# Summing attention rows: GpSimd folds to 16 columns, VectorE adds the rest, and five engines' instruction lists in a new order

## The chip, the cores and the metric

The kernel runs on one core of one Trainium2 chip. The metric is the device time of that core in microseconds (us). An execution is judged as a whole: there is one launch, and every input starts in device memory.

## The reference

128 graphs of 128 nodes with 384 features go through two layers, each with a residual and a layer norm.

```
# L0, twice:  u_left = h (h Wl^T)^T / sqrt(384),  u_right likewise with Wr
#             u = u_left*triu(adj) + u_right*triu(adj,1)^T
#             att = exp(u)*adj / (sum(exp(u)*adj) + 1e-10)
#             h = relu(layer_norm(att @ (h Wlin^T + b)))
x = layernorm(x + L0(x))
# L1, 12 heads of 32:  q,k,v = x Wq^T, x Wk^T, x Wv^T + bv
scores = q k^T * scale + (adj + adj)
row_nonzero = any(scores != 0, axis=-1)          # else the row becomes 0
out = nan_to_num(softmax(scores)) v  @ Wo^T + bo
x = layernorm(x + out)
```

Every product is made of three products of halves (high times high, high times low, low times high), so that 16-bit operands carry nearly full precision. Each value that feeds TensorE is therefore rounded by ScalarE (`_hi`) and its rest is taken by VectorE or GpSimd (`_lo`).

## The kernel before

The 128 graphs are taken in 32 groups of four (`GROUP`). One pass of the program (`body(p)` on each engine) works on L0 of group `it` and on L1 of group `it - 1` at once, and on the last head block, the last output projection and the last layer norm (`TAIL`) of the group before that. Passes 0, 1 and 2 stand as straight code, passes 3 to 30 are a loop of seven rounds with four passes each, and passes 31 to 33 are straight code again. Pass 0 has no L1 work and also rounds weights 2 to 9 (`setup`); pass 32 has only L1 work, pass 33 only the tail.

Each engine has its own list of calls in `body`, written out; an engine does its list strictly in order and meets the others only through semaphores, whose counts `upto` works out. A call is named by its stage and its part:

- L0: `nl(l, c)` the six products of the left and right weights for layer l (nine matmuls of 512 columns each); `hl(l, b)` the linear part of graph b (nine of 384); `u(l, h)` the pair scores of two graphs (18 matmuls of 256 columns); `u_add`, `exp_u`, `weigh`, `round_e`, `e_rest` make the attention weights `e`; `ctx(l, b)` multiplies them on; `den`, `bn`, `z_variance`, `z_power`, `inv_std`, `norm_z` normalise layer 0's result `z`; `th(k)` turns it (four 128x128 transposes).
- L1: `x1t` turns the residual `x1`, `qk(c)` and `v(b)` are projections, `scores(b, c)` the head scores of graph b. On TensorE these are 36 small matmuls per graph into the four banks 4 to 7. VectorE's `scores(b, j)` (line 847) adds the adjacency, writes the negated scores `s` and takes their minimum `nmax`; ScalarE's `exps(b, j)` (line 597) makes the exponentials `w`. Then `pt` (transposes of `w`, three per graph), `pv` (36 matmuls of 33 columns), `rs_of` and `pv` on VectorE (lines 874, 877, 889: divide by the row sum into `o`), `to` (transposes of `o`) and `po` (output projection), and `po_stats`, `y2_power`, `fin` for the last layer norm.

The reference sets a row to zero when all its scores are zero. The kernel tests this by two numbers of each row and head: the maximum, and the sum of `s` over its 128 columns (`total`). GpSimd's `folds(b)` (lines 455 to 473) makes the sum: seven additions of halves, 128 columns to 64, 32, 16, 8, 4, 2 and 1, for 12 heads at once, each waiting for the one before by a semaphore (`fold1` to `fold6`, `s_tot`). VectorE's `live_of(b)` (line 865) takes the larger of the maximum and `total` into `live`, and `rs_of(b)` multiplies the reciprocal by whether that is above zero (line 877). VectorE's `scores(b)` for b of 2 and 3 waits for `fold1` of two graphs earlier, since `s` has two buffers.

The eight PSUM banks are shared by a written list `BANK_USES`: bank by bank, in which order the stages use it. Before a stage writes its bank, TensorE waits in `await_bank` for the last reader of the stage ahead of it in that list (`READ`: for `pt` the rest `pt_lo`, for `pv` the output `o_ok`, and so on). `scores` of a graph waits for all four banks 4 to 7 at its first call. So a reader that comes late on VectorE holds TensorE at the next use of the bank.

The DMA issues (SyncE) are: inputs of the next group, `adj2` for L1, `xres` for the residual, and the stores of finished rows. Their order is the same in both kernels.

Of the kernel before, what the change touches and what calls it, by code (L numbers as in the profile page):

```python
# [5 lines left out]
GROUP = 4  # L6
# [24 lines left out]
def program(nc, x, xT, adj, adjT, weights, biases, ln_cols, ln_rows, out):  # L31
# [5 lines left out]
    with ExitStack() as stack:  # L37
# [62 lines left out]
        def signal(name, per_group):  # L100
# [12 lines left out]
            for p in ("u_full", "u_read", "u_sum", "e_raw", "e_ok", "e_hi_ok", "e_lo_ok"))  # L113
# [16 lines left out]
        fold1, fold2, fold3, fold4, fold5, fold6, s_tot = (  # L130
            signal(p, GROUP) for p in ("fold1", "fold2", "fold3", "fold4", "fold5", "fold6", "s_tot"))
# [15 lines left out]
                     s_full, s_ok, s_tot, fold1, fold2, fold3, fold4, fold5, fold6, p_ok, pt_full, pt_hi, pt_lo, pv_full, live_ok, rcp_ok,  # L147
# [9 lines left out]
        def uses(*runs):  # L157
# [3 lines left out]
            uses(("nl0", 1), ("hl0", 2), ("v", 0), ("pt", 1), ("pv", 0), ("nl1", 4), ("to", 1), ("pv", 2), ("c1", 0)),  # L161
            uses(("to", 3), ("qk", 1, 5), ("th", 1), ("nl1", 0), ("to", 0), ("pt", 5, 6), ("to", 2), ("c1", 1)),
            uses(("pv", 3), ("nl0", 3), ("u0", 1), ("qk", 0, 3), ("th", 0), ("v", 3), ("pt", 0), ("nl1", 2),
                 ("po", 0), ("pv", 1), ("hl1", 1), ("po", 1), ("pt", 10)),
            uses(("nl0", 4), ("x1t", 0), ("qk", 4), ("v", 1), ("th", 2), ("nl1", 3), ("hl1", 0), ("pt", 7),
                 ("u1", 1), ("hl1", 3), ("c1", 2)),
            uses(("hl0", 1), ("x1t", 1), ("c0", 0, 2), ("s", 0), ("v", 2), ("s", 4, 8), ("pt", 4), ("s", 12),
                 ("pt", 8), ("hl1", 2), ("po", 2), ("c1", 3)),
            uses(("nl0", 2), ("hl0", 0), ("x1t", 2), ("c0", 1, 3), ("s", 1, 5), ("nl1", 1), ("s", 9, 13), ("u1", 0)),
            uses(("nl0", 5), ("u0", 0), ("hl0", 3), ("s", 2, 6), ("pt", 2), ("s", 10), ("nl1", 5), ("s", 14),  # L170
                 ("pt", 9)),
            uses(("nl0", 0), ("po", 3), ("qk", 2), ("s", 3, 7), ("pt", 3), ("s", 11, 15), ("pt", 11)))
# [14 lines left out]
        class Pass:  # L187
# [40 lines left out]
            def await_bank(self, eng, stage, *parts):  # L228

                last = {}  # L230
# [102 lines left out]
        def _(pool):  # L333
# [115 lines left out]
            def folds(p, b):  # L449
# [32 lines left out]
            def body(p):  # L482
# [3 lines left out]
                hl(p, 0, 1)  # L486
                out_bias(p, 0)
                weigh(p, 0, 0)
                e_rest(p, 0, 0)
                weigh(p, 0, 1)  # L490
                hl(p, 0, 2)
                e_rest(p, 0, 1)
                out_bias(p, 1)
                hl(p, 0, 3)
                out_bias(p, 2)
                y2_power(p, 3)
                scale_adj(p)
                z_power(p, 0)
                out_bias(p, 3)
                v(p, 0)  # L500
                folds(p, 0)
                folds(p, 1)
                v(p, 1)
                xt(p, 0)
                v(p, 2)
                folds(p, 2)
                xt(p, 1)
                hl(p, 1, 0)
                y2_power(p, 0)
                folds(p, 3)  # L510
                hl(p, 1, 1)
                weigh(p, 1, 0)
                v(p, 3)
                weigh(p, 1, 1)
                e_rest(p, 1, 0)
                e_rest(p, 1, 1)
# [18 lines left out]
        def _(act):  # L535
# [142 lines left out]
            def body(p):  # L678
                nl(p, 0, 0)
                setup(p, 2)  # L680
                setup(p, 3)
                setup(p, 4)
                nl(p, 0, 1)
# [4 lines left out]
                nl(p, 0, 5)  # L688
                x1_norm(p, 2)
                x1_norm(p, 3)  # L690
                hl(p, 0, 0)
# [3 lines left out]
                x1t(p, 1)  # L695
                x1t(p, 2)
                round_e(p, 0, 0)
                exp_u(p, 0, 1)
                fin(p, 2)
                hl(p, 0, 2)  # L700
                qk(p, 0)
                round_e(p, 0, 1)
                hl(p, 0, 3)
                ctx(p, 0, 0)
                qk(p, 1)
                ctx(p, 0, 1)
# [5 lines left out]
                setup(p, 5)  # L712
                qk(p, 5)
                setup(p, 6)
                v(p, 0)
                th(p, 0)
                th(p, 1)
                exps(p, 0, 0)
                exps(p, 0, 1)
                exps(p, 0, 2)  # L720
                th(p, 2)
                exps(p, 0, 3)
                exps(p, 1, 0)
                pt(p, 0, 0)
                exps(p, 1, 1)
# [3 lines left out]
                pt(p, 1, 0)  # L729
                setup(p, 7)  # L730
                nl(p, 1, 1)
                xt(p, 0)
                exps(p, 1, 2)
                nl(p, 1, 2)
                setup(p, 8)
                setup(p, 9)
                v(p, 1)
                fin(p, 3)
                v(p, 2)
                nl(p, 1, 3)  # L740
                to(p, 0)
                exps(p, 1, 3)
                xt(p, 1)
                pt(p, 1, 1)
# [46 lines left out]
        def _(dve):  # L791
# [293 lines left out]
            def body(p):  # L1085
# [3 lines left out]
                scale_z(p, 1)  # L1089
                nl(p, 0, 0)  # L1090
                pv(p, 3)
                nl(p, 0, 1)
                scale_z(p, 2)
                scale_z(p, 3)
                inv_std(p, 1)
                to(p, 3)
                shift_z(p, 0)
# [451 lines left out]
```

## Time and profile before

| | us |
|---|---|
| median of 3 runs | 2906.12 |
| lowest, highest | 2905.11, 2912.86 |
| the profiled execution | 2910.63 |
| its span, first to last instruction | 2908.9 |
| TensorE busy | 2811.0 |
| VectorE busy | 2433.9 |
| ScalarE busy | 1773.5 |
| GpSimd busy | 1662.0 |
| mean granted TensorE clock | 0.987 of full speed |

"Busy" is the time in which an engine has an instruction at work; instructions that only wait, branch or issue transfers don't count. The profile page lists this first, then the span in slices, the queues, the chain of work that ended last, and the costliest groups of instructions with the idle time of the engine ahead of each and what ended it. A matmul's recorded length is longer than the distance to the next one, since they overlap; where the speed of TensorE matters, the distances count.

### The profile page before, as it was taken

How to read it: one execution, taken by the hardware profiler on the slowest of the kernel's cores; microseconds unless marked ns; L12 is line 12 of the kernel's file. 1: busy time of each engine (PE TensorE's matmuls, PEld its weight loads, DVE VectorE, ACT ScalarE, POOL GpSimd, SP SyncE). 2: the span in 40 equal slices, each digit the busy share in tenths (PEclk: the TensorE clock that was granted, in tenths of full speed). 3: DMA queues.
4: the chain of work that ended last, by engine and by line, in shares of the span. 5: the costliest groups of instructions: out<-in, count | busy, mean ns of one | idle time of the engine just before them, and what ended most of it. 6: DMA issues, size and time to landing. Idle time of an engine off the chain costs nothing.

```text
span 2908.9 us, 74992 instructions
## 1 busy us (share of the span) xinstructions
PE 2811.0 (97%) x24768; PEld 1794.6 (62%) x24768; DVE 2433.9 (84%) x8042; ACT 1773.5 (61%) x4107; POOL 1662.0 (57%) x2097
## 2 busy tenths in 40 slices
PE   7999999999999999999999999999999999999996
PEld 4566666666666566665666656666566656666654
DVE  4888988888888789887888878897888888888886
ACT  4565666556676556665566655566565666655664
POOL 2555566556565556664565645656555655556564
PEclk9999999999999999999999999999999999999997
DMA  4001011101011010111110110101101011101000
GB/s 149 30 31 45 21 45 42 42 32 45 21 42 42 32 45 21 45 42 38 36 42 24 43 43 31 45 21 46 39 34 43 31 35 42 42 31 45 21 27 21
DMA packets 56061, 113.03 MB, mean 39 GB/s; under 512 B 4944, under 2 KB 37712, under 8 KB 55632
## 3 DMA queue, kind: packets, MB, share of 16 engines
q1 hardware_dynamic: 55632, 107.76, 11.0%
q8 instruction: 214, 3.51, 0.5%
q14 instruction: 215, 1.76, 0.2%
HBM read 82.58 MB, written 25.17 MB: 37 GB/s over the span
## 4 chain that ended last, share of the span: by engine, by line
PE 80%; DVE 10%; issue 6%; ACT 3%; DVEq 0%; POOL 0%; DMA 0%; SPq 0%; POOLq 0%; ACTq 0%
PE psum L1251 58%; PE psum L1261 9%; PE psum L1312 9%; PE psum L1405 3%; DVE z L1017 2%; PE psum L1379 1%; ACT w L597 1%; DVE nT_lo L814 1%; DVE rs L877 1%; DVE pT_lo L812 1%; DVE hT_lo L1038 1%; DVE o L889 1%; ACT qk_hi L537 1%; ACT pT_hi L537 1%; DVE st L916 1%
## 5 line engine op out<-in xcount | busy, mean ns | idle before, releaser
L597 ACT ACTIVATE w<-s,nmax 128x128 f32<-128x128 f32 x1536 | 479.4, 401 | 1.9 <-DVE nmax L847 1.9
L1251 PE MATMUL psum<-hT_hi,w_hi 128*128 128x512 f16 x1152 | 442.8, 384 | 35.4 <-issue 19.7
L1251 PE MATMUL psum<-hT_hi,w_lo 128*128 128x512 f16 x1152 | 442.3, 384 | 0.0
L1251 PE MATMUL psum<-hT_lo,w_hi 128*128 128x512 f16 x1152 | 442.2, 384 | 0.0
L537 ACT ACTIVATE nT_hi<-psum 128x512 f16<-128x512 f32 x384 | 230.1, 599 | 306.1 <-PE psum L1251 306.1
L847 DVE CUSTOM_DVE_ANT_0 s<-psum,adj 128x128 f32<-128x128 f32 x1536 | 350.6, 285 | 33.3 <-PE psum L1379 30.6
L464 POOL TENSOR_TENSOR fold<-fold 128x384 f32<-128x384 f32 (+4 forms) x640 | 344.0, 538 | 50.2
L464 POOL TENSOR_TENSOR fold<-s 128x768 f32<-128x768 f32 x128 | 244.2, 1908 | 194.7 <-DVE nmax L847 194.7
L388 POOL TENSOR_TENSOR hl_lo<-hl_raw,hl_hi 128x384 fp32r<-128x384 f32 x256 | 246.6, 968 | 144.9 <-ACT hl_hi L537 140.7
L812 DVE TENSOR_TENSOR pT_lo<-psum,pT_hi 128x512 f16<-128x512 f32 x384 | 251.5, 683 | 35.1 <-ACT pT_hi L537 34.7
L537 ACT ACTIVATE pT_hi<-psum 128x512 f16<-128x512 f32 x384 | 221.7, 596 | 84.3 <-PE psum L1261 84.3
L814 DVE SCALAR_TENSOR_TENSOR nT_lo<-psum,nT_hi 128x512 f16<-128x512 f32 x384 | 256.3, 681 | 12.4 <-ACT nT_hi L537 12.3
L431 POOL TENSOR_TENSOR yrstd<-yvar,pw 128x4 f32<-128x4 f32 x32 | 32.4, 1013 | 397.8 <-DVE yvar L997 397.8
L537 ACT ACTIVATE z<-psum,rden 128x384 f32<-128x384 f32 x256 | 138.3, 579 | 197.4 <-DVE rden L963 197.4
L1251 PE MATMUL psum<-w_hi,hT_lo 128*128 128x384 f16 x768 | 250.3, 326 | 0.0
L1251 PE MATMUL psum<-w_lo,hT_hi 128*128 128x384 f16 x768 | 250.3, 326 | 0.0
L1251 PE MATMUL psum<-w_hi,hT_hi 128*128 128x384 f16 x768 | 250.3, 326 | 0.0
L1251 PE MATMUL psum<-xT_hi,w_hi 128*128 128x512 f16 x576 | 219.8, 382 | 0.0
L1251 PE MATMUL psum<-xT_lo,w_hi 128*128 128x512 f16 x576 | 219.1, 380 | 0.0
L1251 PE MATMUL psum<-xT_hi,w_lo 128*128 128x512 f16 x576 | 218.8, 380 | 0.0
L1251 PEld LDWEIGHTS psum<-hT_hi,w_hi 128*128 128x128 f16 x1152 | 113.2, 98 | 165.1 <-issue 43.0
L1261 PE MATMUL psum<-ident,w 128*128 128x128 f32 x1536 | 208.7, 276 | 2.6 <-DVE nmax L847 2.0
(133 smaller groups left out, 8066.6 us busy)
## 6 DMA issues: line engine op xcount, KB each, us to landing
xTin<-xT SPq DMA_DIRECT2D x32, 768.0 KB, 4.5
xres<-x SPq DMA_DIRECT2D x32, 768.0 KB, 4.6
out<-y SPq DMA_DIRECT2D x128, 192.0 KB, 1.9
adjn<-adj SPq DMA_DIRECT2D x32, 256.0 KB, 4.8
adjT_sb<-adjT SPq DMA_DIRECT2D x32, 256.0 KB, 5.0
adj<-adj SPq DMA_DIRECT2D x32, 256.0 KB, 2.7
x<-weights SPq DMA_DIRECT2D x4, 576.0 KB, 5.3
s<-weights SPq DMA_DIRECT2D x3, 576.0 KB, 6.3
```

The costliest lines, as they stand in the source:

```text
L388: nc.gpsimd.tensor_tensor(hl_lo[:, b, 0:FEAT], hl_raw[:, b], hl_hi[:, b, 0:FEAT].bitcast(f32), ALU.subtract).then_inc(hlr_lo[l].sem, 1)
L464: nc.gpsimd.tensor_tensor(fold[:, :, 0:n], src[:, :, 0:n], src[:, :, n:2 * n], ALU.add)\
L537: return nc.scalar.activation(dst, src, ACT.Copy, scale=scale)
L597: last = nc.scalar.activation(w[:, m], s[b % 2][:, m], ACT.Exp, bias=nmax[b % 2][:, m:m + 1], scale=-1.0)
L812: nc.vector.tensor_tensor(dst, src, rounded, ALU.subtract).then_inc(done.sem, 1)
L814: nc.vector.scalar_tensor_tensor(dst, src, scale, rounded, ALU.mult, ALU.subtract)\
L847: last = nc.vector.tensor_tensor_reduce(out=s[b % 2][:, m], in0=psum[:, SC[j], c * TOK:(c + 1) * TOK], in1=adj2[:, b], scale=-1.0 / TEMPER ...
L1017: nc.vector.tensor_scalar(z[:, b], z[:, b], rstd[0][:, b:b + 1], nmr[:, b:b + 1], ALU.mult, ALU.add)\
L1251: last = mm(dst, a, b, start=(i == 0), stop=(i == total - 1))
L1261: last = transpose(dst[:, n * 128:(n + 1) * 128], src, ident[:])
L1312: last = mm(dst, a, m, start=(i == 0), stop=(i == len(terms) - 1))
L1405: last = mm(dst[:, n * VCOL:(n + 1) * VCOL], a, m, start=(i == 0), stop=(i == 2))
```

## The change

`folds(b)` keeps its first three additions (128 columns to 64, 32, 16) and loses the four small ones. VectorE's `live_of(b)` waits for `fold3` and adds the 16 columns left in one `tensor_reduce` over 12 heads, then waits for that and goes on as before. GpSimd's own wait for `s_tot` ahead of its next `folds` stays, and now is released by VectorE.

```diff
@@ folds (GpSimd)
-                for n, src_ok, done in ((TOK // 2, None, fold1), (TOK // 4, fold1, fold2), (TOK // 8, fold2, fold3),
-                                        (TOK // 16, fold3, fold4), (TOK // 32, fold4, fold5),
-                                        (TOK // 64, fold5, fold6)):
+                for n, src_ok, done in ((TOK // 2, None, fold1), (TOK // 4, fold1, fold2), (TOK // 8, fold2, fold3)):
...
-                pool.wait_ge(fold6.sem, p.upto(fold6, b + 1))
-                if b >= 2:
-                    pool.wait_ge(live_ok.sem, p.upto(live_ok, b - 1))
-                elif p.before.l1:
-                    pool.wait_ge(live_ok.sem, p.before.upto(live_ok, b + 3))
-                nc.gpsimd.tensor_tensor(total[b % 2][:], fold[:, :, 0], fold[:, :, 1], ALU.add)\
-                    .then_inc(s_tot.sem, 1)
@@ live_of (VectorE)
+                dve.wait_ge(fold3.sem, p.upto(fold3, b + 1))
+                nc.vector.tensor_reduce(total[b % 2][:], fold[:, :, 0:TOK // 8], AX.X, ALU.add).then_inc(s_tot.sem, 1)
                 dve.wait_ge(s_tot.sem, p.upto(s_tot, b + 1))
@@ scores (TensorE): the wait for qk's rests joins the bank wait of c == 0
-                    p.await_bank(pe, "s", *range(TILES * b, TILES * (b + 1)))
-                if b == 0:
+                    p.await_bank(pe, "s", *range(TILES * b, TILES * (b + 1)), also=(("qk", 1),) if b == 0 else ())
+                elif b == 0:
                     pe.wait_ge(qkr_lo.sem, p.upto(qkr_lo, 2 * c + 2))
```

All four compute engines' lists in `body` and `BANK_USES` are laid out anew; the calls are the same calls. TensorE's list, before and after (parts in brackets, `p` left out):

```
before: nl00 pv3 nl01 nl02 to3 nl03 nl04 po3 nl05 hl00 hl01 u00 u01 x1t0-2 hl02 hl03 qk0 qk1 ctx00 ctx01 qk2
        ctx02 ctx03 qk3 qk4 qk5 v0 th0 sc0(0-2) th1 v1 v2 v3 th2 sc1(0-2) pt00 pt01 nl10 nl11 pt02 pt10 nl12 pv0
        nl13 sc2(0-2) to0 nl14 pt11 pt12 po0 nl15 pv1 hl10 sc3(0-2) to1 hl11 pt20 pt21 pt22 u10 po1 pv2 u11
        pt30 to2 hl12 pt31 hl13 pt32 po2 ctx10-13
after:  nl00 pv3 nl01 nl02 to3 nl03 nl04 nl05 po3 hl00 u00 hl01 u01 hl02 x1t0-2 hl03 qk0 ctx00 ctx01 qk1
        ctx02 ctx03 qk2 qk3 qk4 qk5 th0 th1 v0 sc0(0,1) th2 sc0(2) v1 v2 v3 sc1(0-2) pt00 pt01 nl10 pt02 nl11
        pv0 nl12 sc2(0-2) to0 nl13 pt10 pt11 pt12 nl14 po0 nl15 pv1 pt20 sc3(0-2) hl10 pt21 u10 hl11 pt22 hl12
        pt30 to1 pt31 pv2 u11 pt32 hl13 to2 po1 po2 ctx10-13
```

VectorE's list in the stretches that matter, after (before where it differs in kind):

```
start:   rs3 z_variance1 scale_z0 nl00 pv3 scale_z1 nl01 inv_std1 scale_z2 to3 ...   (before: scale_z1 ahead of nl00)
z:       bn00 den01 bn01 bn02 bn03 z_variance0 qk1 qk2 fin3 inv_std0 norm_z0-3 qk3 qk4 qk5 th0 v0 th1 sc00-03
         (before: ... z_variance0 qk2 qk3 qk4 fin3 inv_std0 norm_z0-3 qk5 v0 sc00-03 th0)
head 1:  v1 v2 v3 th2 sc10 sc11 pt00 pt01 pt02 sc12 live0 rs0 sc13 pv0 nl10 nl11 sc20 sc21 sc22 to0 sc23 nl12
         pt10 pt11 pt12 live1 po0 nl13 nl14 po_stats0 rs1 nl15 pt20 pv1 hl10 sc30 sc31 sc32 u10 sc33 live2 ...
```

ScalarE: `th0 th1 th2` now follow `qk5` directly, ahead of `v0` and of the `exps` of graph 0 (before, `th2` came between them); `exps` of graph 1 follow `pt0x`; `v1`, `v2`, `v3` and `xt2` stand together after `to0`. GpSimd: `weigh` and `e_rest` of both halves are paired, `z_power(0)` is ahead of `y2_power(3)`, `v3` and `xt2` come earlier.

## Rows read from the trace of the kernel before

**Rows 1.** The page's part 1: busy time and share of the span per engine.
```profile
PE 2811.0 (97%) x24768; PEld 1794.6 (62%) x24768; DVE 2433.9 (84%) x8042; ACT 1773.5 (61%) x4107; POOL 1662.0 (57%) x2097
```
**Rows 2.** Busy by stretch: length; PE, PEld, DVE, ACT, POOL; clock, DMA, GB/s.
```profile
1406.80:1494.50 87.70, 86.84 (x775) 55.77 (x774) 75.83 (x252) 54.85 (x128) 51.91 (x66) 1.00 0.12 38
...
530.80:623.20 92.40, 87.35 (x777) 56.03 (x776) 75.40 (x251) 55.09 (x128) 51.93 (x65) 1.00 0.11 37
```
**Rows 3.** Waits of TensorE, 76 to 2759 us: total, times, longest.
```profile
PE psum L1251 <- issue: 19.7, 6, 4.4
PE psum L1261 <- DVE o L889: 18.5, 32, 1.3
PE psum L1261 <- DVE z L1017: 7.9, 30, 0.3
PE psum L1251 <- DVE hT_lo L1038: 1.5, 7, 0.2
```
**Rows 4.** The chain of waits, 1446 to 1478 us: start, length, what.
```profile
1446.23 1.51 DVE z L1017 x4
...
1456.73 0.84 DVE hT_lo L1038
...
1463.20 0.90 PE psum L1405 x36
...
1466.05 0.61 PE psum L1379 x36
...
1467.14 1.94 PE psum L1251 x9
1469.08 0.45 PE psum L1261 x4
...
1475.13 1.05 DVE rs L877
...
1477.43 1.46 PE psum L1251 x9
```
**Rows 5.** TensorE's instructions in order of time, around `th0` and inside `nl10`.
```profile
1447.36 0.33 PE L1251 MATMUL psum<-w_hi,xT_lo 128*128 128x384 f16 x1
1447.94 0.66 PE L1261 MATMUL psum<-ident,z 128*128 128x128 f32 x4 [0.25 <-DVE z L1017]
...
1457.17 0.38 PE L1251 MATMUL psum<-hT_hi,w_lo 128*128 128x512 f16 x1
1457.62 0.39 PE L1251 MATMUL psum<-hT_hi,w_hi 128*128 128x512 f16 x1
```
**Rows 6.** Groups of GpSimd by shape: busy, mean ns; idle before.
```profile
L464 POOL TENSOR_TENSOR fold<-fold 128x96 f32<-128x96 f32 x128 | 50.0, 391 | 10.0
L464 POOL TENSOR_TENSOR fold<-fold 128x48 f32<-128x48 f32 x128 | 45.7, 357 | 10.0
...
L464 POOL TENSOR_TENSOR fold<-fold 128x24 f32<-128x24 f32 x128 | 30.8, 241 | 10.0
L472 POOL TENSOR_TENSOR total<-fold 128x12 f32<-128x12 f32 x128 | 26.9, 210 | 10.6 <-POOL fold L464 1.1
```
**Rows 7.** Single lines of VectorE: duration ns min/median/max, first and last start.
```profile
L874 DVE RECIPROCAL rs<-psum x128: 208/226/234, 131.7 to 2897.9; 128x12 f32<-128x12 f32 x128
```
**Rows 8.** The same view, the statistics of 384 columns.
```profile
L970 DVE BATCH_NORM_STATS2 st<-z x256: 540/554/562, 38.2 to 2829.8; 128x6 f32<-128x384 f32 x128
```
**Rows 9.** The same view, `live`, and `rs` at line 877.
```profile
L865 DVE SCALAR_TENSOR_TENSOR live<-nmax,total x128: 156/163/1000, 130.3 to 2896.7; 128x12 f32<-128x12 f32 x128
L877 DVE SCALAR_TENSOR_TENSOR rs<-live,rs x128: 170/172/1130, 132.0 to 2898.2; 128x12 f32<-128x12 f32 x128
```
**Rows 10.** VectorE in order of time: rests of 512 columns, one after the other.
```profile
1481.32 1.88 DVE L812 TENSOR_TENSOR pT_lo<-psum,pT_hi 128x512 f16<-128x512 f32 x3
```
**Rows 11.** VectorE in order of time: the scores of part 3 of graph 0.
```profile
1451.46 0.29 DVE L847 CUSTOM_DVE_ANT_0 s<-psum,adj 128x128 f32<-128x128 f32 x1
...
1452.10 0.08 DVE L847 DVE_READ_ACCUMULATOR2_ANT nmax<- 128x1 f32 x1
```
**Rows 12.** Waits of TensorE, 2825 us to the end.
```profile
PE psum L1261 <- DVE o L889: 6.9, 4, 4.1
PE psum L1261 <- DVE x L1065: 6.6, 1, 6.6
PE psum L1251 <- DVE oT_lo L812: 3.6, 3, 1.2
```
**Rows 13.** The first fold of each graph on GpSimd, durations as in Rows 7.
```profile
L464 POOL TENSOR_TENSOR fold<-s x128: 1806/1816/2210, 119.8 to 2887.0; 128x768 f32<-128x768 f32 x128
```

More of the change, by code:

```diff
@@ L129, in program @@
         s_full, s_ok, p_ok = (signal(p, GROUP * TILES) for p in ("s_full", "s_ok", "p_ok"))
-        fold1, fold2, fold3, fold4, fold5, fold6, s_tot = (
-            signal(p, GROUP) for p in ("fold1", "fold2", "fold3", "fold4", "fold5", "fold6", "s_tot"))
+        fold1, fold2, fold3, s_tot = (signal(p, GROUP) for p in ("fold1", "fold2", "fold3", "s_tot"))
         pt_full, pt_hi, pt_lo = (signal(f"pt_{p}", GROUP * KB) for p in ("full", "hi", "lo"))
@@ L226, in await_apart, with await_bank @@
                 eng.wait_ge(sig.sem, value)
-            def await_bank(self, eng, stage, *parts):
-                last = {}
+            def await_bank(self, eng, stage, *parts, also=()):
+                last = {name: (self.group(READ[name]), i) for name, i in also}
                 for i in parts:
@@ L486, in body @@
                 hl(p, 0, 1)
-                out_bias(p, 0)
[L488 to L492, printed above, removed]
+                weigh(p, 0, 0)
+                weigh(p, 0, 1)
+                e_rest(p, 0, 0)
+                e_rest(p, 0, 1)
+                hl(p, 0, 2)
+                hl(p, 0, 3)
+                out_bias(p, 0)
                 out_bias(p, 1)
-                hl(p, 0, 3)
-                out_bias(p, 2)
-                y2_power(p, 3)
                 scale_adj(p)
                 z_power(p, 0)
+                y2_power(p, 3)
+                v(p, 0)
+                out_bias(p, 2)
                 out_bias(p, 3)
-                v(p, 0)
                 folds(p, 0)
@@ L711, in body @@
                 qk(p, 4)
-                setup(p, 5)
                 qk(p, 5)
-                setup(p, 6)
-                v(p, 0)
                 th(p, 0)
                 th(p, 1)
+                th(p, 2)
+                v(p, 0)
                 exps(p, 0, 0)
                 exps(p, 0, 1)
+                setup(p, 7)
                 exps(p, 0, 2)
-                th(p, 2)
                 exps(p, 0, 3)
-                exps(p, 1, 0)
+                fin(p, 3)
                 pt(p, 0, 0)
-                exps(p, 1, 1)
+                xt(p, 0)
                 pt(p, 0, 1)
@@ L728, in body @@
                 nl(p, 1, 0)
-                pt(p, 1, 0)
-                setup(p, 7)
+                exps(p, 1, 0)
                 nl(p, 1, 1)
-                xt(p, 0)
+                exps(p, 1, 1)
                 exps(p, 1, 2)
[L734 to L741, printed above, removed]
                 exps(p, 1, 3)
                 xt(p, 1)
+                to(p, 0)
+                xt(p, 2)
+                v(p, 1)
+                setup(p, 8)
+                v(p, 2)
+                nl(p, 1, 2)
+                v(p, 3)
+                setup(p, 9)
+                pt(p, 1, 0)
+                nl(p, 1, 3)
                 pt(p, 1, 1)
@@ L1088, in body @@
                 scale_z(p, 0)
-                scale_z(p, 1)
                 nl(p, 0, 0)
                 pv(p, 3)
+                scale_z(p, 1)
                 nl(p, 0, 1)
+                inv_std(p, 1)
                 scale_z(p, 2)
-                scale_z(p, 3)
-                inv_std(p, 1)
-                to(p, 3)
-                shift_z(p, 0)
-                shift_z(p, 1)
+                to(p, 3)
+                nl(p, 0, 2)
+                shift_z(p, 0)
+                setup(p, 2)
+                shift_z(p, 1)
+                resid(p, 0)
+                resid(p, 1)
+                y_bn(p, 0)
+                setup(p, 3)
+                y_bn(p, 1)
+                scale_z(p, 3)
+                nl(p, 0, 3)
+                nl(p, 0, 4)
+                nl(p, 0, 5)
+                setup(p, 4)
+                po(p, 3)
                 shift_z(p, 2)
                 shift_z(p, 3)
-                nl(p, 0, 2)
-                resid(p, 0)
-                resid(p, 1)
-                po(p, 3)
-                y_bn(p, 0)
-                y_bn(p, 1)
-                setup(p, 2)
-                setup(p, 3)
-                setup(p, 4)
-                nl(p, 0, 3)
                 resid(p, 2)
                 resid(p, 3)
-                nl(p, 0, 4)
-                nl(p, 0, 5)
                 y_bn(p, 2)
@@ L1480, in body @@
                 to(p, 0)
-                nl(p, 1, 4)
+                nl(p, 1, 3)
+                pt(p, 1, 0)
                 pt(p, 1, 1)
                 pt(p, 1, 2)
+                nl(p, 1, 4)
                 po(p, 0)
```

201 lines of the change are left out of this document (100 added, 101 removed).

## The prediction, made before the changed kernel was run

> **What bounds the kernel now.** I read the busy shares first, then a table of busy time by stretch, then TensorE's waits, then the chain of waits through one pass, and at last its instructions one by one. TensorE is busy for 2811.0 of 2908.9 us [rows 1]. A pass in the middle takes 87.70 us and TensorE is at work in 86.84 of them; VectorE in 75.83, ScalarE in 54.85, GpSimd in 51.91 [rows 2]. So TensorE's own work bounds the pass and 12 us of VectorE's time are free, but not freely placed. The waits say where TensorE loses time between 76 and 2759 us: 18.5 us for `o`, 7.9 for the normalised `z`, 1.5 for the rests `hT_lo` of layer 1, and 19.7 us with the mark "issue", six times up to 4.4 us [rows 3]. Those six are the jumps of the loop: such a stretch takes 92.40 us in place of 87.70 [rows 2], the change adds or takes away no jump, and I leave them as they are.
>
> Idle time tells less than the loss, since a matmul overlaps the next. At `th0` the last matmul of `v0` starts at 1447.36 and the transposes at 1447.94 [rows 5], 0.58 us later; nine such matmuls take 1.46 us [rows 4], 0.16 each. The loss is 0.42 us where the wait shows 0.25. In `nl10` two matmuls are 0.45 us apart [rows 5], where nine take 1.94 [rows 4], 0.22 each: 0.23 us lost to `hT_lo` in every pass, of which the waits show nearly nothing.
>
> **The change, part by part.**
>
> GpSimd loses four additions per graph: 391 + 357 + 241 + 210 ns and four waits of 10.0/128 = 0.08 us [rows 6], 1.5 us per graph, 6.1 per pass. It is busy 51.91 of 87.70 us [rows 2] and no wait in rows 3 names it. Worth nothing by itself.
>
> VectorE gains one `tensor_reduce` of 192 columns to 12 per graph and one wait for itself. No row shows this operation. The nearest are a one-input operation of 12 columns, 0.226 us [rows 7], and one that reads 384 and writes 6, 0.554 us [rows 8]. By columns between them it is 0.226 + 0.328 x 180/372 = 0.38 us. Lower end 0.23; upper end 1.0, the longest that the equally placed `live` ever took [rows 9]. I take 0.38, as it lies between two rows that hardly vary, and 0.10 for the wait, after the 0.08 between two folds on GpSimd: 0.48 per graph, 1.9 us per pass, of 11.9 free. VectorE then has 77.7 of some 86.5 us at work. Queued behind it is its whole list: `rs`, the next scores, `o`.
>
> The long `live` and `rs` are the second point: 163 and 172 ns in the median, 1000 and 1130 at most [rows 9], and one `rs` of 1.05 us stands in the chain right ahead of the `o` that TensorE waits for [rows 4]. Both read two operands from SBUF, while the statistics with one input never leave 540 to 562 ns [rows 8].
>
> The Trainium skill explains it (SBUF — State Buffer, "Who interferes with whom"): a VectorE instruction with two SBUF inputs and a GpSimd instruction that reads SBUF exclude each other, and `tensor_reduce` never takes part in that on this chip. The spread of rows 8 and 9 agrees. By that rule the upper end of 1.0 us is excluded. Another page speaks against the change (VectorE: DVE Perf Modes, "Rules for kernel authors"): `tensor_reduce` runs at the plain rate and is called the slowest operation of the engine, to be restructured on a hot path. No run here shows it yet.
>
> The order is the larger part. TensorE has the same instructions, so only its waits can move. Its stages last, from rows 4: `nl`, `qk` 1.94; `hl`, `v`, `po` 1.46; `scores` of a graph 0.61; four transposes 0.45; `pv` 0.90. On VectorE a rest of 512 columns takes 1.88/3 = 0.63 us in a row [rows 10], a part of the scores 0.7 [rows 11], an `o` 0.5. I go through the places where TensorE waits, and those where the new lists make one due sooner.
>
> 1. `z` before `th0`. Cover on TensorE after the last `ctx0`: three `qk` and `v0` before, 7.28 us; four `qk` now, 7.76. On VectorE `inv_std` had three `qk` rests ahead since the variance and has two and a tiny `fin` now, 0.6 us less. The margin moves by 1.1 us against a loss of 0.42: gone, with some 0.6 to spare. The small extra distance behind `th0` (about 0.1) goes with it. GpSimd's `y2_power` now stands between, 0.56 us by my estimate, beside the rests of `qk1` and `qk2`.
> 2. `hT_lo` before `nl10`. `th2` was followed by `scores` and two `pt`, 1.5 us; now by the last third of a `scores`, three `v`, `scores`, two `pt`: 0.2 + 4.4 + 0.6 + 0.9 = 6.1. The 0.23 us go.
> 3. `o1` before `to1`. The cover was `hl10` and `scores`, 2.1 us; the chain is `rs` 0.23 + 0.17 (or 1.05) + `o` 0.57 with gaps of 0.1. Now nine stages stand between. But bank 3 goes from `pv1` to `u10`, so `o1` is due at `u10`, after `pt20`, `scores`, `hl10`, `pt21`: 0.45 + 0.61 + 1.46 + 0.45 = 3.0 us. VectorE does `rs1`, `nl15`, `pt20`, `o1` in 0.5 + 0.6 + 0.6 + 0.5, with the first gap 2.4. Spare 0.6; a long `rs` eats it.
> 4. `o0` before `to0`: `nl12` and `scores`, 2.55 us; VectorE has `rs0` 0.5, `scores(1,3)` 0.7, `o0` 0.5: 1.7 to 1.9, spare 0.7. The scores of graph 2 need `scores(1,3)` out of bank 7: 1.94 against 1.3, spare 0.6.
> 5. `live0` stands ahead of `rs0` and `scores(1,3)` and waits for `fold3`. Counted from `th0`, VectorE has read graph 0's scores at 7 us; GpSimd is through `v0`, `out_bias2` and `3` at about 8.6, and three folds of 1.8 + 1.0 + 0.7 and two gaps end at 12.3. VectorE reaches `live0` at 13.4: spare 1.1.
> 6. `x1t` is pushed back by one `hl` (1.46) and VectorE's list ahead of it grows by `u00` and `u_add00` less `hl01`, 0.6: safer. `o3` comes one `scale_z` (0.6) earlier.
> 7. ScalarE drops back by some 4 us behind TensorE at `nl12`, since four `exps` and two `xt` stand ahead. Only the rests behind it are due, `nl13` at `pv1` and `nl14` at `hl10`, and both are spare by 0.7 or more.
>
> So every wait that I find goes and none is left without at least half a microsecond. The sum, 30 passes: `o` 18.5 + `z` 7.9 [rows 3], the hidden part of `z` 30 x 0.17 = 5.1, `hT_lo` 30 x 0.23 = 6.9: 38.4 us. I give back 0.25 us per pass, 7.5 in all, for places 3 and 4, where spares of 0.6 meet the spread of rows 9. That leaves 31 us. Head: two roundings of weights now stand ahead of ScalarE's first `ctx`, +1. Tail: TensorE waits for `o`, `x` and `oT_lo` for 6.9 + 6.6 + 3.6 us [rows 12]; `pv` comes before graph 1's last `pt` and the exponentials of graph 2 start earlier, against 2 us more on VectorE: -3. Sum -33 us. The profiled execution took 2910.63, so 2878 by that; the median of the runs is 4.5 lower, and on its scale I forecast 2874.
>
> **Rivals.**
>
> B, half of it comes back: spares of 0.6 are my sums over lists of 20 entries, and each operation can be late by what rows 9 show. If places 3 and 4 lose 0.35 us each on average, 31 x 0.45 more than I gave: 2888 to 2895, say 2890.
>
> C, the time stays: what the new lists free at `th0`, `nl10` and `to1` is met again at the next bank, because VectorE was 86% busy in a pass and is 90% now. For it: its waits are few and short, it hardly ever rests between `o3` and `x1t`. Against: a rest frees one bank, and TensorE stands at the new dues at least 0.6 later. Time 2906, within 2897 to 2915. What differs from before by less than 0.3%, 8.7 us, I call no change.
>
> D, slower: VectorE gets behind at `live_of`. Place: `live0` to `live3`, each with the scores of the next graph and `o` queued behind. Price: if the reduction takes 1.0 us, or waits so long for `fold3`, 0.6 x 4 = 2.4 us more per pass in front of dues with 0.6 spare: about 2.0 us arrive at TensorE, less the 1.3 gained: +0.6, 31 passes +19: 2925. It decides from about 1.1 us per `live_of` instead of 0.48. For it: `live` itself took up to 1.0 [rows 9], and the first fold up to 2.21 [rows 13]. Against: a one-input operation never did [rows 8].
>
> By the skill's rule that it is the slowest operation D would hold with the same 2925; by the other rule it would not.
>
> E, the change doesn't do what it says: the fold is still what `live` waits for, only with three steps. That would be seen as VectorE waiting at the reduction; its time is within C.
>
> **How the numbers follow.** A, the forecast: 0.58, own range 2864 to 2887. B 0.14. C with E 0.12. D 0.16. Faster 0.58 + 0.14 = 0.72, same 0.12, slower 0.16. The lower end is the whole 38 us and 5 of the tail, 2906 - 43, rounded to 2862; the upper end takes in B and C, 2914. Outside are D and a few hundredths below.
>
> **What would show it.** A middle pass of 86.2 to 86.6 us with VectorE at 77 to 78. Waits of TensorE for `o` and `z` of a few microseconds in all; "issue" near 20 with six entries. Distance from the last matmul ahead of `th0` to the transposes near 0.2 us. The reduction at 0.3 to 0.45 us without spread, and no wait of VectorE on GpSimd's fold. GpSimd's busy time down by 153 us. Wrong would be: `fold` as a releaser of VectorE with tens of microseconds, TensorE waiting before `u10`, before the scores of graph 2 or before `to0`, or VectorE's busy time per pass above 79 us.

## The result, and the profile after

The changed kernel takes 2878.41 us (median of 4 runs, 2876.72 to 2879.57), the kernel before 2907.42 on the same chip: a ratio of 0.9897 with a 95% interval of 0.9881 to 0.9913, 1% faster. The profiled execution took 2876.72, its span is 2875.0 us against 2908.9. The medians are 29.0 us apart and the two profiled executions 33.9: the profiled one of the kernel before was 3.2 us above its median, that of the changed kernel 1.7 below. The lists of TensorE, VectorE, ScalarE and GpSimd are new; SyncE's is the same in both kernels, so it is four engines and not five, as the title has it.

The page's first part, as in [rows 1]:

```profile
PE 2805.5 (98%) x24768; PEld 1791.6 (62%) x24768; DVE 2468.7 (86%) x8170; ACT 1787.8 (62%) x4107; POOL 1492.4 (52%) x1585
```

TensorE does the same 24768 matmuls. GpSimd is at work 170 us less, VectorE 35 more, and the span is 33.9 shorter. Of the 170, the four additions are 153. The rest is a difference between operations of GpSimd that run shorter in the new order, as the first fold (1.82 us on average, 1.91 before), and some that run longer. Next the busy time by stretch, with the columns of [rows 2]: a middle pass, one with a jump of the loop in it, then the first 3.1 us of such a jump and the 2.0 us behind it.

```profile
1407.80:1494.60 86.80, 86.80 (x776) 55.76 (x774) 76.87 (x256) 55.43 (x128) 46.55 (x49) 1.00 0.11 38
...
528.60:619.10 90.50, 87.20 (x776) 55.87 (x775) 76.88 (x255) 55.55 (x128) 46.56 (x49) 1.00 0.12 37
...
1299.10:1302.20 3.10, 0.09 (x1) 0.00 (x0) 2.86 (x10) 2.07 (x4) 3.10 (x4) 1.00 0.04 8
1302.20:1304.20 2.00, 1.95 (x9) 0.90 (x10) 0.18 (x1) 0.71 (x1) 0.16 (x1) 1.00 0.10 29
```

In the middle pass TensorE never rests. The same view of the kernel before, at the same jump:

```profile
1311.90:1316.50 4.60, 0.37 (x3) 0.05 (x1) 3.10 (x11) 2.81 (x5) 3.38 (x4) 0.77 0.05 11
1316.50:1320.40 3.90, 3.83 (x10) 1.37 (x11) 0.00 (x0) 0.00 (x0) 0.00 (x0) 0.50 0.18 61
```

And the instruction that TensorE starts with behind the jump, of the kernel before and then of the changed one, in order of time with the wait at the end:

```profile
1316.57 0.61 PE L1251 MATMUL psum<-hT_hi,w_hi 128*128 128x512 f16 x1 [4.29 <-issue]
```
```profile
1302.25 0.39 PE L1244 MATMUL psum<-hT_hi,w_hi 128*128 128x512 f16 x1 [3.06 <-issue]
```

Before, TensorE stood still for 4.29 us and then ran the nine matmuls of `nl00` at a granted clock of 0.50, which is 1.2 GHz, in 3.8 us. After, it stood still for 3.06, was granted 1.00 (2.4 GHz), and the same nine took 1.95.

The shorter stop alone doesn't explain the clock. Two jumps later in the changed kernel TensorE stood for only 2.52 us and was granted 0.50 behind it:

```profile
2004.31 0.60 PE L1244 MATMUL psum<-hT_hi,w_hi 128*128 128x512 f16 x1 [2.52 <-issue]
```

TensorE's waits between 79 and 2723 us, as in [rows 3] ("issue" marks idle time for which the profile shows nothing that was awaited):

```profile
PE psum L1244 <- issue: 16.7, 6, 3.1
PE psum L1398 <- issue: 0.7, 1, 0.7
```

The waits for `o`, `z` and `hT_lo` of [rows 3] are gone. VectorE's new operation and the two behind it, durations as in [rows 9], and what GpSimd waits for ahead of its first fold (total, times, longest):

```profile
L856 DVE TENSOR_REDUCE total<-fold x128: 334/342/350, 129.7 to 2855.7; 128x12 f32<-128x192 f32 x128
L858 DVE SCALAR_TENSOR_TENSOR live<-nmax,total x128: 170/170/173, 130.1 to 2856.1; 128x12 f32<-128x12 f32 x128
L870 DVE SCALAR_TENSOR_TENSOR rs<-live,rs x128: 170/172/1049, 130.9 to 2863.2; 128x12 f32<-128x12 f32 x128
```
```profile
POOL fold L462 <- DVE nmax L838: 146.0, 32, 4.9
POOL fold L462 <- DVE total L856: 86.7, 64, 2.1
```

To see where the 33.9 us come from I measured the distance of one pass to the next at the same instruction of VectorE, the last step of the variance of the residual (`yvar`, line 997 before, 990 after):

| | before | after | difference |
|---|---|---|---|
| to the first such instruction | 92.69 | 94.96 | +2.3 |
| 25 passes without a jump | 2188.2 (87.53 each) | 2166.2 (86.65 each) | -22.0 |
| 6 passes with a jump | 560.53 | 544.80 | -15.7 |
| from the last one to the end | 67.43 | 69.03 | +1.6 |

(The 25 hold the first passes and the last ones, which have less to do.) So 0.88 us per pass, which would be 5.3 of the 15.7 at the jumps; the other 10.4 us are the jumps' own.

The granted clock accounts for most of these. Around the jumps TensorE worked 22.8 us at 0.50 before, at five of the six, and 8.9 us after, at three of them. Half of such time is lost, as with the nine matmuls above: an estimate of 11.4 and 4.5 us. Its stops add up to 19.7 and 16.7 us. Together that is 10 us less.

### The profile page after: what moved, and what is told of

It is laid out like the page before. It is cut to its first block, busy times and chain, and to the rows that moved or that the text cites. A ratio compares the mean times of both kernels' runs of the same rounds, so it can differ in the third digit from the quotient of the medians.

```text
span 2875.0 us, 74223 instructions
## 1 busy us (share of the span) xinstructions
PE 2805.5 (98%) x24768; PEld 1791.6 (62%) x24768; DVE 2468.7 (86%) x8170; ACT 1787.8 (62%) x4107; POOL 1492.4 (52%) x1585
## 4 chain that ended last, share of the span: by engine, by line
PE 96%; issue 1%; DVE 1%; ACT 1%; DMA 0%; POOL 0%; SPq 0%; POOLq 0%; DVEq 0%; ACTq 0%
PE psum L1244 70%; PE psum L1254 11%; PE psum L1305 9%; PE psum L1398 4%; PE psum L1372 3%; DMA xTin<-xT 0%; DMA s<-weights 0%; ACT w L588 0%; ACT w_hi L528 0%; DVE st L963 0%; POOL hl_lo L388 0%; DVE w_lo L786 0%; DVE st L909 0%; DVE y L901 0%; POOL e L417 0%
## 5 line engine op out<-in xcount | busy, mean ns | idle before, releaser
L1244 PE MATMUL psum<-hT_hi,w_hi 128*128 128x512 f16 x1152 | 441.2, 383 | 29.5 <-issue 16.7
L462 POOL TENSOR_TENSOR fold<-s 128x768 f32<-128x768 f32 x128 | 232.6, 1817 | 232.7 <-DVE nmax L838 146.0
L528 ACT ACTIVATE hl_hi<-hl_raw 128x384 fp32r<-128x384 f32 x256 | 133.1, 520 | 308.2 <-DVE hl_raw L818 308.2
L396 POOL TENSOR_TENSOR v_lo<-v_raw,v_hi 128x384 f16<-128x384 f32 x128 | 112.5, 890 | 279.8 <-ACT v_hi L528 279.8
L462 POOL TENSOR_TENSOR fold<-fold 128x384 f32<-128x384 f32 (+1 forms) x256 | 218.0, 851 | 20.1
L1254 PE MATMUL psum<-ident,w 128*128 128x128 f32 x1536 | 221.7, 278 | 3.9 <-DVE nmax L838 1.8
```

The lines of the kernel that those rows point to most:

```text
L396: nc.gpsimd.tensor_tensor(v_lo[:, b, :, 0:HEAD], v_raw[:, b].rearrange("p (h d) -> p h d", h=HEADS), v_hi[:, b, :, 0:HEAD], ALU.subtract). ...
L528: return nc.scalar.activation(dst, src, ACT.Copy, scale=scale)
L1244: last = mm(dst, a, b, start=(i == 0), stop=(i == total - 1))
L1254: last = transpose(dst[:, n * 128:(n + 1) * 128], src, ident[:])
```

## The experiments

Ratios are to the kernel before, run beside on the same chip; "a pass" is the median distance of two passes without a jump, 87.73 us before and 86.87 after.

**after_again**: the changed kernel once more.

> The changed kernel once more, on the chip and in the rounds of the next three, so that they can be set against it. 2876 to 2881 us; plain passes 86.8 to 86.9 us, loop crossings 90 to 91.5 us. If the shorter crossings of its first profile (sum of six 544.8 us, against 560.6 before) were luck of one execution, they will be near 93 us here.

Measured 2879.85 us, ratio 0.9899 [0.9884, 0.9915], a pass 86.87. The gain stands. The six jumps took 90.1 to 92.4 us, 546.6 in all, with 14.5 us of TensorE's work at half clock, at four of them. So the clock at the jumps differs between two executions of one kernel, and this sum is 1.8 us longer.

**fold_only**: the new sums in the old order, that is the first two hunks of the diff of `folds` and `live_of` on the kernel before.

> The old order with the new sums: three folds on GpSimd, the reduction in VectorE's live_of. Theory 1 (the order makes the gain, the sums alone cost): VectorE's 0.34 us reduction and its wait, 0.4 us together, stand right ahead of rs1 and o1, for which TensorE already waits 0.54 us; so that wait grows by 0.4 us, and to3, which had 0.24 us to spare, waits up to 0.2 us. Plain passes 88.1 to 88.4 us, 2918 to 2930 us. Theory 2 (the relief of GpSimd makes the gain, by fewer collisions of two-input VectorE operations with it): plain passes 87.0 to 87.5, 2885 to 2900 us, and the mean of rs at line 870 or so falls below its 374 ns.

Measured 3008.5 us, ratio 1.0338 [1.0323, 1.0352], a pass 91.03. Missed by 80 us: alone, the new sums cost 3.4%. The waits of TensorE from 79 to 2850 us, then VectorE's `rs` with its durations, then GpSimd's first fold by shape with the idle time ahead of it:

```profile
PE psum L1253 <- DVE o L881: 77.7, 83, 1.5
PE psum L1243 <- issue: 20.4, 6, 4.5
PE psum L1243 <- DVE hl_raw L817: 9.3, 30, 0.4
```
```profile
L869 DVE SCALAR_TENSOR_TENSOR rs<-live,rs x128: 170/1058/1610, 132.1 to 2999.3; 128x12 f32<-128x12 f32 x128
```
```profile
L461 POOL TENSOR_TENSOR fold<-s 128x768 f32<-128x768 f32 x128 | 244.0, 1907 | 589.2 <-DVE total L855 528.6 <-DVE nmax L837 60.5
```

The reduction itself is 0.34 us as in the changed kernel, but `rs` on 12 columns takes 1.06 us in the median against 0.17 [rows 9]. All engines in order of time show how:

```profile
1441.45 0.35 DVE L855 TENSOR_REDUCE total<-fold 128x12 f32<-128x192 f32 x1
1441.83 0.17 DVE L857 SCALAR_TENSOR_TENSOR live<-nmax,total 128x12 f32<-128x12 f32 x1
1441.87 1.82 POOL L461 TENSOR_TENSOR fold<-s 128x768 f32<-128x768 f32 x1 [4.52 <-DVE total L855]
1441.92 0.23 DVE L866 RECIPROCAL rs<-psum 128x12 f32<-128x12 f32 x1
1442.17 1.54 DVE L869 SCALAR_TENSOR_TENSOR rs<-live,rs 128x12 f32<-128x12 f32 x1
1443.77 1.00 POOL L461 TENSOR_TENSOR fold<-fold 128x384 f32<-128x384 f32 x1
1443.82 0.56 DVE L881 TENSOR_TENSOR o<-psum,rs 128x384 f32<-128x384 f32 x1
```

GpSimd had stood for 4.52 us because the next graph's folds wait for `s_tot`, which VectorE now releases. The reduction lets it go, its fold of 1.82 us starts 0.07 us later, and `rs`, three instructions on, doesn't end before that fold does (1443.69 and 1443.71). `o` and TensorE stand behind. The one that frees GpSimd is held by what it frees. All 96 of the 128 `rs` that took over 0.4 us end with a GpSimd instruction, within 0.06 us.

**order_only**: the new order with the old seven folds.

> The new order with the old sums: seven additions on GpSimd, none on VectorE. Theory 1: the order keeps most of the gain, and what the shorter sums buy is room on GpSimd at the end of the pass: its folds of graph 3 end 0.1 us before VectorE takes them up and are followed by weigh, e_rest and hl of layer 1, the last of which ends about 0.8 us before ctx13 needs it; 1.5 us more make TensorE wait for hl_lo or e_lo by 0.5 to 1.2 us in a pass. 2890 to 2912 us. If the sums were without any use in the new order: 2872 to 2880 us, since VectorE has 1.6 us less in a pass. Theory 2: no gain at all, 2903 to 2912 us with waits for o and z as before.

Measured 2876.15 us, ratio 0.9889 [0.9874, 0.9904], a pass 86.7. Missed: I had thought that the order needs the room on GpSimd, and it doesn't. Its median is 3.7 us below the changed kernel's, and the intervals overlap: the whole gain is the order's, and the new sums add nothing to it. In a pass they cost 0.17 us; `rs` takes 0.18 us on average here and 0.43 in the changed kernel.

**fold_2buf_old**: `fold_only`, but the third fold writes one of two small tiles, so that GpSimd need not wait for the reduction of the graph before.

```diff
-                    pool.wait_ge(s_tot.sem, p.upto(s_tot, b))
+                    pool.wait_ge(fold3.sem, p.upto(fold3, b))
...
-                    nc.gpsimd.tensor_tensor(fold[:, :, 0:n], src[:, :, 0:n], src[:, :, n:2 * n], ALU.add)
+                    dst = last16[b % 2][:] if done is fold3 else fold[:, :, 0:n]
+                    nc.gpsimd.tensor_tensor(dst, src[:, :, 0:n], src[:, :, n:2 * n], ALU.add)
```

> fold_only (old order, new sums), but the third fold writes its 16 columns into one of two tiles, so that GpSimd starts the folds of the next graph without VectorE's reduction of the last. Theory R (release): fold_only lost 3.3 us in a pass because the reduction releases GpSimd's next first fold, 1.8 us long, at the very moment when rs follows on VectorE, and rs with its two SBUF inputs is held until that fold ends (0.98 us in the mean in place of 0.37). Without the release plain passes are 88.1 to 88.6 us and the time is 2915 to 2932 us, rs back at 0.35 to 0.5 us. Theory V (VectorE's added work as such, behind a list with no spare): nothing changes, plain passes 90.5 to 91.1 us, 2990 to 3010 us.

Measured 2891.09 us, ratio 0.9935 [0.9921, 0.995], a pass 87.43. The direction is right and the size too timid: the release costs 117 us in the old order, and without it the new sums gain 0.65%. `rs` and TensorE's waits (79 to 2730 us):

```profile
L877 DVE SCALAR_TENSOR_TENSOR rs<-live,rs x128: 170/171/887, 131.6 to 2880.5; 128x12 f32<-128x12 f32 x128
```
```profile
PE psum L1251 <- issue: 17.9, 6, 4.0
PE psum L1261 <- DVE z L1017: 7.9, 30, 0.3
PE psum L1261 <- DVE o L889: 0.4, 2, 0.2
```

The 18.5 us for `o` of [rows 3] are gone here, the 7.9 for `z` stay as they were.

**fold_2buf_new**: the same two tiles in the new order.

> The same two tiles in the changed kernel. There GpSimd waits for reductions too, but rs is long only for graph 1 (0.92 us), and the 0.1 us that TensorE loses at pt21 is behind it. Theory R: rs falls from 0.43 us to 0.2 to 0.4, plain passes 86.7 to 86.85 us in place of 86.87, 2873 to 2880 us. Theory V: no change at all, 2877 to 2881 us.

Measured 2909.27 us (11 runs), ratio 1.0001 [0.9992, 1.001], a pass 87.72. Missed: the remedy takes the whole gain away. The first wait of TensorE (79 to 2750 us), `live`, and all engines in order of time:

```profile
PE psum L1262 <- DVE hl_raw L826: 21.5, 30, 1.1
```
```profile
L866 DVE SCALAR_TENSOR_TENSOR live<-nmax,total x128: 170/172/1691, 131.6 to 2889.1; 128x12 f32<-128x12 f32 x128
```
```profile
1482.20 1.80 POOL L470 TENSOR_TENSOR fold<-s 128x768 f32<-128x768 f32 x1 [1.70 <-DVE nmax L846]
1482.36 1.68 DVE L866 SCALAR_TENSOR_TENSOR live<-nmax,total 128x12 f32<-128x12 f32 x1
```

In this order the freed fold begins 0.16 us ahead of `live` of graph 2 and holds it for 1.68 us; `hl_raw` is copied late, and the `pt` behind it on TensorE waits 0.7 us, every pass. So the wait for the reduction, 86.7 us of GpSimd's time in the changed kernel, is of use there: it keeps the fold behind `live`.

**fold_only_psum**: `fold_only`, with the reciprocal written into 12 unused columns of `pv`'s PSUM bank, so that `rs` reads only `live` from SBUF.

```diff
-                nc.vector.reciprocal(rs[b % 2][:], src[:, :, HEAD])
+                rcp = bank("pv", b)[:, HEADS * VCOL + 4:HEADS * VCOL + 4 + HEADS]
+                nc.vector.reciprocal(rcp, src[:, :, HEAD])
...
-                nc.vector.scalar_tensor_tensor(rs[b % 2][:], live[b % 2][:], 0.0, rs[b % 2][:], ALU.is_gt, ALU.mult)
+                nc.vector.scalar_tensor_tensor(rs[b % 2][:], live[b % 2][:], 0.0, rcp, ALU.is_gt, ALU.mult)
```

> fold_only (old order, new sums, one fold tile), but the reciprocal in rs_of is written to 12 free columns of pv's own PSUM bank, and rs reads it there. rs then has one SBUF input. Everything else, the release of GpSimd's next fold by the reduction too, stays. Theory R (the released fold holds rs because both read SBUF by the shared path): rs falls from 0.98 us to 0.17 to 0.25, the waits for o shrink from 90.6 us to below 35, plain passes 87.5 to 89 us, 2895 to 2945 us. If the release costs by GpSimd's lateness and not by holding rs: rs is short but the waits stay, plain passes above 90 us, 2980 us or more. If rs stays long although it has one SBUF input, it isn't held by that fold.

Measured 2958.79 us, ratio 1.0173 [1.0157, 1.0188], a pass 89.52: half of what `fold_only` lost, and between the two cases that I had set. VectorE's `rs` by shape (busy, mean, idle ahead) and TensorE's waits (79 to 2800 us):

```profile
L870 DVE SCALAR_TENSOR_TENSOR rs<-live,psum 128x12 f32<-128x12 f32 x128 | 21.4, 167 | 4.6 <-DVE psum L867 0.2
```
```profile
PE psum L1244 <- DVE hl_raw L817: 34.1, 30, 1.2
...
PE psum L1254 <- DVE o L882: 11.7, 22, 0.9
```

A change of where one operand lies takes `rs` from 0.98 us on average to 0.167, under the same folds: 97 of the 128 start while a GpSimd instruction is running, and all take 166 to 168 ns. That is the pattern which the Trainium skill states (SBUF — State Buffer, "Who interferes with whom"): VectorE and GpSimd exclude each other only where VectorE needs its second, shared port. The other half has moved to `hl_raw`. `live` is held as before (0.41 us on average), but the order of time shows GpSimd, which still waits 481 us for the reduction, at the start of this chain:

```profile
1506.27 1.82 POOL L461 TENSOR_TENSOR fold<-s 128x768 f32<-128x768 f32 x1 [3.07 <-DVE total L855]
1511.47 0.42 ACT L527 ACTIVATE e_hi<-e 128x256 fp32r<-128x256 f32 x1 [2.63 <-POOL e L416]
1512.30 0.56 DVE L802 TENSOR_TENSOR oT_lo<-psum,oT_hi 128x384 f16<-128x384 f32 x1 [2.81 <-ACT oT_hi L527]
1513.47 0.32 PE L1244 MATMUL psum<-w_hi,oT_hi 128*128 128x384 f16 x1 [1.13 <-DVE hl_raw L817]
```

GpSimd's last folds start late, its `weigh` comes behind them, ScalarE stands for `e` with `oT_hi` behind it in its list, and VectorE stands for `oT_hi` with `hl_raw` behind. ScalarE waits for `e` 120.0 us in all here and 122.8 in `fold_only`, against 38.7 in the kernel before and 38.6 in `fold_2buf_old`, which has the new sums without the release. So the release costs in two ways: half by holding `rs`, and the rest mainly by making GpSimd late. No run takes away that second part alone.

**reduce_more4**: four more reductions of the same kind in each `live_of` of the changed kernel.

> The changed kernel with five reductions in live_of in place of one (the four more write a tile that nobody reads): 4 x 0.27 to 0.34 us more of VectorE ahead of live in every graph, 4.3 to 5.4 us in a pass, VectorE at 82 to 84 of 87 us. It measures the spare of the new order. My rival D of the prediction said that above 1.1 us per live_of, in place of 0.48, TensorE gets 2.0 us of a further 2.4; here live_of takes about 1.7 us: plain passes 88.5 to 91 us, 2925 to 3000 us. If the spares were much larger than the half microsecond that I worked out: below 2895 us.

Measured 2926.24 us, ratio 1.0055 [1.0039, 1.0071], a pass 88.11, the six with a jump 564.1. The time is at the lower edge, a pass below it. Busy time of a middle pass:

```profile
1430.00:1518.10 88.10, 87.44 (x775) 55.34 (x774) 79.93 (x272) 55.54 (x128) 46.51 (x49) 1.00 0.11 37
```

In a row the reductions start 0.26 us apart, since their records overlap, so sixteen more are 4.2 us and not 5.4; a pass grows by 1.24. VectorE's slack takes up the rest, and its busy time grows by 3.1.

**unroll14**: the changed kernel with two loop rounds of 14 passes, one jump in place of six.

```diff
-            with eng.Fori(3, GROUPS - 4, 4) as it:
-                for n in range(4):
+            with eng.Fori(3, GROUPS - 14, 14) as it:
+                for n in range(14):
```

> The changed kernel with 14 passes in a round of the loop in place of 4, two rounds in place of seven: one crossing in place of six, all else the same. If a crossing costs what the profile shows (90.8 us in place of 86.9), five of them less are worth 19 us: 2857 to 2862 us. If the gaps come from reading in instructions as such, and straight code of this length has them too, the time stays at 2878 us within 5.

Measured 2855.09 us, ratio 0.9813 [0.98, 0.9827], just below the range: 24.8 us for five jumps, 5.0 each. In the profile of `after_again` a pass with a jump is only 4.2 us longer than the others. A part of the difference lies in the passes without one, 86.80 us here in place of 86.87.

**straight_order**: `order_only` with every pass as straight code.

> The new order with the old sums, and all 34 passes as straight code, no loop. unroll14 took away five crossings and 24.8 us; this takes away the sixth (4.6 us there) and has the 3.7 us of order_only: 2855 less 4.6 less 3.7, 2845 to 2849 us. If straight code of this length meets gaps of its own in reading in instructions, it is 2855 us or more.

Measured 2845.45 us, ratio 0.9779 [0.9765, 0.9793]. Between 79 and 2720 us TensorE waits for nothing, its granted clock is never below 1.00 there, and a pass takes 86.61. Against `order_only` that is 30.7 us for six jumps, 5.1 each.

**straight_order_psum**: this with the PSUM reciprocal.

> straight_order with the same change of rs. There rs is 0.24 us in the mean, so there is at most 0.07 us to gain on it, and TensorE waits for nothing in a plain pass of 86.61 us: 2842 to 2847 us, the same as straight_order within the noise. It is the candidate for the fastest version.

Measured 2845.19 us, ratio 0.9781 [0.9768, 0.9794]: the same. `rs` is 0.167 us without spread, but nothing waits for it any more. These two are the fastest versions, 33 us below the changed kernel.

**th2_back**: the changed kernel, with `th2` behind `v3` on TensorE, and on ScalarE behind the third part of graph 0's `exps`.

> The changed kernel with th2 put back on TensorE behind v3 and on ScalarE behind the third exps of graph 0, as before the change. Step 2 of the prediction: the third part of nl10 gets its rest too late again, 0.2 to 0.3 us in a pass: plain passes 87.05 to 87.2 us in place of 86.87, 2884 to 2890 us. If step 2 is wrong and another move freed nl10, plain passes stay at 86.87.

Measured 2904.06 us (10 runs), ratio 0.9985 [0.9976, 0.9994], a pass 87.67. TensorE's first wait (79 to 2750 us):

```profile
PE psum L1254 <- ACT hT_hi L631: 29.9, 30, 1.0
```

Missed: `nl10` loses nothing, but `pt00` has the bank behind `th2` and waits 1.0 us for ScalarE's rounding. As that wait stands ahead of `nl10`, it could hide what `nl10` would have lost.

**qk_ahead**: VectorE takes the rests of `qk3` and `qk4` ahead of `inv_std`.

> The changed kernel with the rests of qk3 and qk4 ahead of inv_std on VectorE, as before the change. It tests step 1. In the changed kernel z ends 0.95 us before th0 starts. The rest of qk4 can't start before ScalarE has rounded it, and ends 2.7 us later than inv_std started, so z comes about 2.6 us later and th0 waits 1.5 to 1.9 us: plain passes 88.4 to 88.8 us, 2925 to 2940 us. If z has nothing to do with the gain: no change.

Measured 2935.96 us, ratio 1.0096 [1.008, 1.0111], a pass 88.8. TensorE's wait for `z` (79 to 2750 us), and VectorE's two moved rests in order of time:

```profile
PE psum L1254 <- DVE z L1010: 51.2, 30, 1.7
```

```profile
1456.35 0.69 DVE L805 SCALAR_TENSOR_TENSOR qk_lo<-psum,qk_hi 128x512 f16<-128x512 f32 x1 [0.73 <-ACT qk_hi L528]
1458.29 0.69 DVE L805 SCALAR_TENSOR_TENSOR qk_lo<-psum,qk_hi 128x512 f16<-128x512 f32 x1 [1.25 <-ACT qk_hi L528]
```

As expected. The two rests bring not only their own 1.3 us but waits for ScalarE, so that VectorE comes to `inv_std` 4.71 us after the variance (1454.26 to 1458.97) in place of 1.94. Of the 2.8 us more, 0.95 were to spare (below), and 1.8 are left; TensorE waits 1.7 at `th0`, every pass.

## Why the prediction was right, and where it wasn't

The forecast of 2874 in 2862 to 2914, faster with 0.72, holds: 2878.41, a gain of 29.0 us between medians. By its own steps:

**Step 1** holds, with more to spare than I said. TensorE in the changed kernel:

```profile
1428.45 0.38 PE L1244 MATMUL psum<-xT_hi,w_lo 128*128 128x512 f16 x1
1428.67 1.04 PE L1254 MATMUL psum<-ident,z 128*128 128x128 f32 x8
```

The transposes follow 0.22 us behind the last matmul of `qk5`, the engine's own pace, where [rows 5] had 0.58 behind `v0`; and `z` is ready 0.95 us ahead, where I had 0.6. `qk_ahead` confirms it from the other side.

**Step 2** holds in its result: the 0.23 us inside `nl10` are gone, its matmuls start 0.22 us apart throughout. That the move of `th2` did it isn't shown. What putting `th2` back costs, 0.80 us per pass, is another wait than these 0.23; the place of `th2` is worth more here than the loss I saw.

**Step 3** holds, but its spare of 0.6 us is 0.15. VectorE and TensorE around `o1` and `u10`:

```profile
1456.68 0.92 DVE L870 SCALAR_TENSOR_TENSOR rs<-live,rs 128x12 f32<-128x12 f32 x1
1458.73 0.54 DVE L882 TENSOR_TENSOR o<-psum,rs 128x384 f32<-128x384 f32 x1
```
```profile
1458.88 0.64 PE L1254 MATMUL psum<-ident,w 128*128 128x128 f32 x4
1459.42 0.27 PE L1305 MATMUL psum<-nT_hi,hT_hi 128*128 128x256 f16 x1
```

A long `rs` of 0.92 us eats it, as step 3 said, and `o1` ends 0.15 us ahead of `u10`. So the line "none is left without at least half a microsecond" was wrong here.

**Steps 4 to 7**: none of their dues shows a wait of TensorE between 79 and 2723 us. Their spares weren't measured.

**The sums**: the reduction takes 0.342 us without spread, where I took 0.38 between ends of 0.23 and 1.0. A middle pass has VectorE at 76.87 us, where I had 77.7. A pass of 86.87 lies above my sign of 86.2 to 86.6, which didn't contain even what my own sum gives, 87.70 less 31/30 = 86.67. The spread of `live` is gone in the changed kernel (170 to 173 ns) but `rs` keeps its own. The Trainium skill's other rule (VectorE: DVE Perf Modes, "Rules for kernel authors"), that `tensor_reduce` is the slowest operation, changed nothing at this size, 0.342 us an operation. Rival D, VectorE behind at `live_of`, fell by its condition: the reduction took 0.342 us and not 1.0, and VectorE never waited for the fold. Its price was too high as well: it had 2.4 us more at `live_of` bring 2.0 to TensorE, and in `reduce_more4` 4.2 us more bring 1.24 per pass.

**Terms that were mis-sized.** I gave the passes -31 us and they gave -37.8, of which 10.4 are the jumps' own and weren't in my sum. The rest is below the forecast: 0.88 us each for my 1.03, or 27 us. To see where, I summed the distances from each matmul to the next, start to start, by kind of matmul, over 20 passes without a jump of either kernel. In a pass the scores ahead of `to1` give 0.50 us, the products of 384 columns 0.28 and the `th` behind them 0.15, `nl` 0.28, others 0.05: 1.26 in all, where my terms for `o`, `z` and `hT_lo` were 1.28. What came back is 0.25 us at the transposes of `w` and 0.09 at `ctx`, 0.34 where I gave back 0.25. Of the 0.25, 0.10 is `pt20`, behind which scores now follow, and 0.11 is absent in `order_only`, so it belongs to the new sums.

"I leave them as they are", said of the jumps, is the step that failed: they are 10.4 us shorter in this pair of profiles, and the clock, which I had put at nothing, is most of it. One of them, shown above, has a stop 1.2 us shorter and a clock that doesn't fall for the matmuls behind it, 1.9 us more. In the first one before, the clock had stayed and TensorE waited 1.3 us for `o`, whose `rs` stood on "issue" for 4.5 us on VectorE. Whether the new order has a part in it isn't settled: no run changed the jumps alone, `after_again` has 14.5 us of work at half clock where the same kernel had 8.9, and `fold_2buf_old`, in the old order, has 15.1 with stops of 17.9 us, both below the 22.8 and 19.7 of the kernel before.

Head and tail went the other way: +2.3 for my +1, +1.6 for my -3, 6 us in all (in `after_again` +1.8 and +0.4). In the tail (2780 us to the end) TensorE's waits for `o` and `x` are no smaller than in [rows 12]:

```profile
PE psum L1254 <- DVE o L882: 8.3, 3, 4.0
PE psum L1254 <- DVE x L1058: 6.9, 1, 6.9
```

So the total of -33.9 meets my -33 because the 10 us of the jumps stand against 4 in the other passes and 6 in head and tail; between the medians it is -29.0.

**What I didn't see at all**: that handing the last step of the sum to VectorE also hands it the release of GpSimd's next fold. In the changed kernel TensorE sees at most the 0.17 us per pass by which `order_only` is shorter; in the old order it is the largest effect of the case. I had the spread of `rs` in my rows and took it as a given, not as something whose moment the change decides.

## What to carry to other kernels

When a step moves to another engine, look at the releases that move with it, and at what starts in the same microsecond: a short operation of VectorE with two inputs from SBUF can wait for a whole operation of GpSimd, and what stands behind GpSimd's late work waits too. Put one input into PSUM, or keep the two apart by order; and measure each half of a change by itself, since here the order gains the whole 1% while the sums lose 3.4% without it. Where TensorE's waits are near nothing, count the loop's jumps next: they were worth as much again as the whole change.

## What the runs showed of the hardware

- `rs` on 12 columns takes 0.17 us alone and up to 1.61 us while GpSimd adds 768 columns; `live` up to 1.69. With one input in PSUM `rs` is 0.167 on average. `tensor_reduce` of 192 columns stays within 341 to 349 ns in `fold_only`, where 31 of the 128 start while a GpSimd instruction is running.
- A jump of the loop costs 5.0 to 5.1 us, of which TensorE stands 2.5 to 4.5 on "issue". Behind some jumps the granted clock is 0.50 and behind others it stays at 1.00, and the length of the stop doesn't tell which: behind 4.29 us it fell, behind 3.06 it did not, behind 2.52 it fell. The same kernel had it at three jumps in one execution and at four in another; without jumps (`straight_order`) it stayed at 1.00 from 79 to 2720 us.
- TensorE's shortest distance between kinds of matmul grows where full transposes and the small score matmuls alternate, by about 0.1 us each time (0.56 against 0.44 us from `pt20` to what follows). The kernel before has it too, at `th0` and `th2`.
